# DVE's norm and statistics steps become chunks of their own between the score units, four of them in two halves

## The reference

```python
x = x + tanh(g_xattn[0]) * L0_xattn(layernorm(x), ctx, ctx)   # 16 heads of 8, 512 keys
x = x + tanh(g_ffn[0])   * L0_ffn(layernorm(x))               # 8 experts, top 1, hidden 512
x = x + tanh(g_xattn[1]) * L1_xattn(layernorm(x), ctx)        # self-attention (256 keys), add, norm;
                                                              # cross-attention (512 keys), add, norm;
                                                              # 128 -> 512 -> 128 with relu, add, norm
x = x + tanh(g_ffn[1])   * L1_ffn(layernorm(x))               # rmsnorm, causal self-attention with
                                                              # rotary embedding, rmsnorm, 4 experts, top 2
```

## Time and profile before

| | |
|---|---|
| median of 3 runs | 1208.27 us (1203.97 to 1213.19) |
| the profiled execution's own time | 1199.09 us |
| its span, first to last instruction | 1197.3 us |
| mean granted TensorE clock | 0.941 of full speed |
| PE busy | 1058.3 us (88%) |
| DVE busy | 791.6 us (66%) |
| ACT busy | 620.4 us (52%) |
| POOL busy | 370.3 us (31%) |

### The profile page before, as it was taken

One profiled execution on the slowest core, in us unless ns is written; L12 is line 12 of the kernel. 1 busy time (PEld: TensorE's weight loads), 2 busy tenths in 40 slices (PEclk: granted clock), 3 DMA queues, 4 the chain that ended last, 5 costly groups with the idle time before them and its releaser, 6 DMA issues. The chain is left out here.

```text
span 1197.3 us, 25289 instructions
## 1 busy us (share of the span) xinstructions
PE 1058.3 (88%) x8548; PEld 651.4 (54%) x8548; DVE 791.6 (66%) x1935; ACT 620.4 (52%) x1331; POOL 370.3 (31%) x982
## 2 busy tenths in 40 slices
PE   4999998799998797788899998987988889899998
PEld 1455554477554585444455544444555667656665
DVE  4688887534867424677688869688574776645443
ACT  1477665455664454565477755655544445543221
POOL 4333332221434323434333324322242434200000
PEclk9999998899986898898899998999979899999999
DMA  6655644453434572656655544433334456201000
GB/s 160 192 159 175 176 148 137 153 174 112 130 109 135 161 227 61 192 155 190 193 169 172 158 134 141 136 109 115 106 118 131 125 158 181 75 22 45 10 27 10
DMA packets 173174, 157.98 MB, mean 132 GB/s; under 512 B 13075, under 2 KB 146835, under 8 KB 172691
## 3 DMA queue, kind: packets, MB, share of 16 engines
q1 hardware_dynamic: 168854, 141.24, 39.8%
q0 software_dynamic: 4192, 15.12, 4.0%
HBM read 91.56 MB, written 66.85 MB: 132 GB/s over the span
## 5 line engine op out<-in xcount | busy, mean ns | idle before, releaser
L1102 ACT ACTIVATE prob<-ps 128x512 f32<-128x512 f32 (+1 forms) x768 | 398.9, 578 | 171.5 <-PE ps L1664 128.6
L1296 DVE TENSOR_REDUCE nmax<-ps 128x1 f32<-128x512 f32 x512 | 328.5, 684 | 88.8 <-PE ps L1629 86.8
L1664 PE MATMUL ps<-Qst,Kst 75*128 75x256 bf16 x1408 | 244.4, 285 | 8.6 <-DMA Qst<-mrow 5.8
L1680 PE MATMUL av_ps<-prob,Vx 128*32 128x256 f32 (+1 forms) x3072 | 218.3, 401 | 0.0
L1629 PE MATMUL ps<-Kst,Qst 72*128 72x512 bf16 x512 | 198.2, 403 | 21.7 <-DVE nmax L1296 19.5
L1664 PEld LDWEIGHTS ps<-Qst,Kst 75*128 75x128 bf16 x1408 | 137.0, 102 | 76.4 <-ACT prob L1102 11.8
L1680 PEld LDWEIGHTS av_ps<-prob,Vx 128*32 128x32 f32 x3072 | 92.8, 115 | 67.7 <-issue 38.7
L1026 POOL TENSOR_TENSOR mparts<-nmax,zeros 128x8 bf16<-128x8 f32 x122 | 24.8, 203 | 311.8 <-issue 305.1
L1305 DVE TENSOR_REDUCE nmax<-ps 128x2 f32<-128x512 f32 x128 | 85.9, 687 | 48.5 <-PE ps L1643 47.7
L1106 ACT ACTIVATE OT<-av_ps 128x256 f32<-128x256 f32 x128 | 49.2, 385 | 116.4 <-PE av_ps L1680 116.1
L1629 PEld LDWEIGHTS ps<-Kst,Qst 72*128 72x128 bf16 x512 | 50.5, 99 | 102.2 <-DVE nmax L1296 47.6
(11 more groups left out here) (198 smaller groups left out, 1667.0 us busy)
## 6 DMA issues: line engine op xcount, KB each, us to landing
q_parts<-qp SPq DMA_DIRECT2D x96, 192.0 KB, 2.6
Qst<-q_parts SPq DMA_DIRECT2D x128, 144.0 KB
k_parts<-kp SPq DMA_DIRECT2D x46, 384.0 KB, 3.4
Kst<-k_parts SPq DMA_DIRECT2D x60, 288.0 KB
k_parts<-kp SPq DMA_DIRECT2D x48, 192.0 KB, 2.7
Kst<-k_parts SPq DMA_DIRECT2D x64, 144.0 KB
ctxT<-in_ctxT SPq DMA_DIRECT2D x16, 256.0 KB, 4.8
xs_rows<-in_blank SPq DMA_DIRECT2D x22, 128.0 KB, 4.0
```

What stands on the lines that cost most here:

```text
L1102: act.activation(prob[:, RING_AT[st] % RING, half * 512:half * 512 + w], bank(x)[:, 0:w], ACT.Exp).then_inc(drained(x), 1)
L1296: ve.tensor_reduce(nmax[:, g, u, h % GH:h % GH + 1], bank(st), AX.X, ALU.max, negate=True).then_inc(drained(st), 1)
L1664: last = pe.matmul(o, Ks[0:KROWS, par, h, t * P:t * P + P], Qst[0:KROWS, par, h, :], start=True, stop=not a.rope)
L1680: last = pe.matmul(av_ps[VW * hh:VW * hh + VW, SQ - w:SQ], Vx[:, par, t, h, :], prob[:, place, off * SQ:off * SQ + w], start=(t == 0), sto ...
```

## The change

A second tuple of kinds, `STRINGS`, names the twelve DVE steps above, and `body` opens a chunk at each of them as well. `weave` now has more chunks to place: a string goes to a gap by itself, and the places of the PE steps in the same slot shift too. A step that follows a string and is not of either tuple (a load or a store) goes with the string. Four strings of the feed-forward block become two steps of two tiles each; `f.center` and `f.scale` begin with a `drain`, so each half has one. The arithmetic is the same.

```diff
+STRINGS = ("resid", "stat", "center", "apply", "xstat", "xapply", "f.stat", "f.center", "f.scale", "f.gate", "f.again", "f.rms")
...
         put(n, 14, ("f.stat", i, 0))
-        put(n, 15, ("f.center", i, None))
-        put(n + 1, 0, ("f.scale", i, None))
+        for half in range(2):
+            put(n, 15, ("f.center", i, half))
+        for half in range(2):
+            put(n + 1, 0, ("f.scale", i, half))
...
-        put(n + 1, 5, ("f.again", i, None))
+        for half in range(2):
+            put(n + 1, 5, ("f.again", i, half))
...
-        put(n + 1, 8, ("f.rms", i, None))
+        for half in range(2):
+            put(n + 1, 8, ("f.rms", i, half))
...
             for st in items[p] + [st for st in tiles[0] if st[0] != "m0.h" and per == 1]:
-                if st[0] in MISC_KINDS:
+                if st[0] in MISC_KINDS or st[0] in STRINGS:
                     chunks.append([])
                 chunks[-1].append(st)
...
+            def part_of(t, half):
+                return range(t) if half is None else range(half * t // 2, (half + 1) * t // 2)
...
-            def scale_shift(L, dst, src, shift, t):
-                for i in range(t):
+            def scale_shift(L, dst, src, shift, t, half=None):
+                for i in part_of(t, half):
...
                 elif kind == "f.rms":
                     ve.wait_ge(f_rstd, f_stat(n, 2))
-                    scale_rms(LF, f_out, f_res, "g1", BT).then_inc(f_normed, 1)
+                    last = scale_rms(LF, f_out, f_res, "g1", BT, arg)
+                    if arg == 1:
+                        last.then_inc(f_normed, 1)
```

More of the change, by code:

```diff
@@ L1212, in stats_of, with apply_norm @@
                 return last
-            def apply_norm(L, dst, src, t):
-                for i in range(t):
+            def part_of(t, half):
+                return range(t) if half is None else range(half * t // 2, (half + 1) * t // 2)
+            def apply_norm(L, dst, src, t, half=None):
+                for i in part_of(t, half):
                     last = ve.tensor_scalar(dst[:, i, :], src[:, i, :], L["mv"][:, i, 0:1], L["rstd"][:, i:i + 1],
@@ L1219, in apply_norm, with center_gain @@
                 return last
-            def center_gain(L, dst, src, gain, t):
-                for i in range(t):
+            def center_gain(L, dst, src, gain, t, half=None):
+                for i in part_of(t, half):
                     ve.scalar_tensor_tensor(out=dst[:, i, :], in0=src[:, i, :], scalar=L["mv"][:, i, 0:1],
                                             in1=vecs[:, VI[gain], :], op0=ALU.subtract, op1=ALU.mult)
-            def scale_shift(L, dst, src, shift, t):
-                for i in range(t):
+            def scale_shift(L, dst, src, shift, t, half=None):
+                for i in part_of(t, half):
                     last = ve.scalar_tensor_tensor(out=dst[:, i, :], in0=src[:, i, :], scalar=L["rstd"][:, i:i + 1],
@@ L1232, in scale_shift, with scale_rms @@
                 return last
-            def scale_rms(L, dst, src, gain, t):
-                for i in range(t):
+            def scale_rms(L, dst, src, gain, t, half=None):
+                for i in part_of(t, half):
                     last = ve.scalar_tensor_tensor(out=dst[:, i, :], in0=src[:, i, :], scalar=L["rstd"][:, i:i + 1],
@@ L1508, in ffn_step @@
                     ve.drain()
-                    center_gain(LF, f_res, f_res, "ffn_g", BT)
+                    center_gain(LF, f_res, f_res, "ffn_g", BT, arg)
                 elif kind == "f.scale":
@@ L1512, in ffn_step @@
                     ve.drain()
-                    scale_shift(LF, f_res, f_res, "ffn_b", BT)
+                    scale_shift(LF, f_res, f_res, "ffn_b", BT, arg)
                 elif kind == "f.gate":
@@ L1519, in ffn_step @@
                     ve.wait_ge(f_rstd, f_stat(n, 1))
-                    apply_norm(LF, f_res, f_res2, BT)
+                    apply_norm(LF, f_res, f_res2, BT, arg)
                 elif kind == "f.rms":
                     ve.wait_ge(f_rstd, f_stat(n, 2))
-                    scale_rms(LF, f_out, f_res, "g1", BT).then_inc(f_normed, 1)
+                    last = scale_rms(LF, f_out, f_res, "g1", BT, arg)
+                    if arg == 1:
+                        last.then_inc(f_normed, 1)
             def moe1_step(kind, n, arg):
```

## The result

The changed kernel takes **1230.67 us** (median of five runs, 1220.42 to 1236.06), the kernel before 1208.27 beside it. The ratio is **1.0175, with an interval of 1.0126 to 1.0224**: 1.75% slower, or 21 us. The forecast was a small gain, 1204 us, and the range ended at 1221. The prediction is wrong in its sign.

The account below looks back on a forecast made before the run. PE, busy 88% of the span, was taken as the bound, so only its waits or low-clock time could be won. Gains of 14.3 us less losses of 9.7 made 4.6 us off 1208.27, about 1204 us; own range 1196 to 1210, with rivals 1188 to 1221.

Parts of the forecast that it names:

- The clock: Whole kernel: one stretch at the low clock fewer, as at 197.0, 4 us won; ends 14 us won or lost.
- Gain 1, blocks: Feed-forward blocks: halved strings let reductions come earlier, 4 us; `f.nT` of item 24 behind AV and S, 1.3; together 5.3.
- Gain 2, single strings: Reductions move ahead of single strings, so PE waits less: 3 us in `att1`, 2 in `att0` and `att2`; ends 0 and 15.
- Loss 1, xn: Items 8 to 13: `xapply` waits behind the slot's first reduction, so PE waits longer at `xT`; 4.1 us, ends 0 and 5.
- Loss 2, POOL's queue: Items 10 to 12: later `resid` delays POOL's root, gathers, split and `maxT` by 0.6 us each; 1.8 us lost.
- Loss 3, the copy of V in `att3`: Items 25 to 30, slot 6: `apply` behind a reduction delays V's copy, which `nT` needs; 3.3 us lost, ends 0 and 4.
- Loss 4: Slots 0 and 4 of `att1`: `maxT` moves behind the second S; 0.5 us lost, ends 0 and 2.
- The second, lost cover: Rival: strings lose DVE's idle time under E, with more low-clock stretches in `att1` and `att3`; 19 us slower, 1227 us, chance 0.14.
- The first, waits that only move: Rival: PE waits for DMA landings and POOL in place of banks; gains about 9, losses 9.7; 1209 us, chance 0.22.
- The fourth, all bank waits gone: Rival: all 41.5 us of PE's waits for DVE's score reductions go; 1167 us, chance 0.03.
- The sum: Terms in `att1` without clock: losses 4.1 for xn, 1.8 for POOL's queue, 0.5 for `maxT`, against 3 us gained by single strings.

## Why the prediction was wrong, point by point

- **The clock** is the step that failed. It was taken as 4 us won, one low stretch fewer, because the longest waits become shorter. Measured in the two traces, the time at the low level rose from 141 us to 0.068 / 0.5 x 1218.6 = 166, which costs up to 12 us, and PE's busy time rose by 10.9; over all timed executions the cost is up to 14 to 18 us. The sign of the term was wrong, and with it 16 us or more of the 26 between forecast and result: the term was worked out at one place (197.0, in `att0`), while `att1`, at 0.85 already, has several waits of 0.5 to 1.2 us in each item, and the change made more of them longer than shorter. The upper end, four stretches more or 14 us, holds the traces' 12 but hardly what all executions show.
- **Gain 1, blocks, 5.3 us.** Blocks alone gave 0.9987 (0.9948 to 1.0027), 1.6 us less, and between 6.3 less and 3.3 more: not seen, though an effect of that size isn't quite excluded. Item 22 is not shorter but 1.9 us longer, with DVE busy 35.77 us against 34.89 and the clock at 0.87 against 1.00. Where DVE is nearly saturated, order gave nothing that can be seen. The Trainium skill advises the opposite there (Perfetto Trace Analysis, Optimizing Scalar/DVE Operations: group the work where the engine is saturated). The trace agrees as far as it goes: in halves the item needs 0.9 us more of DVE.
- **Gain 2, single strings, 5 us.** Not found. With `att1` left out, blocks, `att0`, `att2` and `att3` together gave 1.0004 (0.9973 to 1.0035), where the terms without `att1` (gains 7.3, loss 3.3) made 4 us less. In `att1` the bank waits fell by 2.5 us, near the 3 that were taken, but no further than they differ between executions of one order. At the place in item 12 the gain was waited for again at the next landing, as the prediction said of that item and then did not carry through. Whether the other stages gained something that the clock took back (13 us more at the low level, up to 6.5 us) is not clear of the noise.
- **Loss 1, xn, 4.1 us.** The mechanism is as forecast, DVE idle ahead of a reduction with `xapply` behind it, and xn's wait rose by 6.7 us, above the upper end of 5. Its price is another matter: `xapply` alone raised the wait by 4.0 us and cost 0.07% (-0.29 to 0.43).
- **Loss 2, POOL's queue, 1.8 us.** Probably too small: `resid` alone costs 0.64%, some 8 us, and in its trace the parts and landings take 19.7 us of PE's time in `att1`. In the trace of the whole change they rose from 10.1 to 13.6, which is hardly clear of the 13.0 of an unchanged `att1`.
- **Loss 3, the copy of V in `att3`, 3.3 us.** Didn't show: items 24 to 30 went from 172.40 to 168.10. In its place stands what the prediction missed, `apply` at the end of `att1`, behind not one reduction but several (2.48 us): 3.2 us of waits in the whole change and 5 us on item 15; by itself 0.48%, with 3 us on that item.
- **Loss 4** is too small for these traces; all shifts of PE's steps together cost 0.45% (0.16 to 0.74) by themselves.
- **The rivals.** The second, lost cover, at 1227 us with a chance of 0.14, is what happened, with its mechanism and its clock term, in `att1` but not in `att3`. Its test was there to be read, and the earlier trace rows show only one place of it: whether DVE stood idle ahead of most of these strings was not counted. The first, waits that only move, describes the bank waits well and takes in no clock. The fourth, all bank waits gone, would have given 1167 us. The Trainium skill's other rule in the same section, to break up Vector's work where it isn't saturated and makes others idle, met both its conditions here; the measurement, 1.75% slower, speaks against it and decides.
- **The sum** for `att1` as the prediction had it (losses 6.4, gain 3) was 3.4 us; `att1` alone measures 17 us (13 to 21). About two thirds of it is the clock by the traces, and up to 16 us by the granted clock of all its executions.

What stays open: how exactly the loss splits between clock and waits, since low-level time in which PE waits costs less than half of itself; by what pattern of waits the new order of strings lowers the clock; and whether `xapply` really costs more in company than alone.

## What to carry to other kernels

An engine that isn't the bound has useful idle time, and work that stands ahead of a reduction may be in it: before a string is moved behind one, look whether the engine was idle at the string's start, and how many reductions stand there, not one. Trade waits at banks for waits at results only after asking what each is followed by; in item 12 a bank wait won ahead of a landing that was late anyway was worth nothing. And where the bound is TensorE, set the busy time of the same matmuls beside each other first: here half of the loss or more was matmuls that ran at the lower clock, and no table of waits shows that. Do it with more than one execution: the trace with the change everywhere but in `att1`, a kernel as fast as the one before, has PE busy 1082.2 us and 189 us at the low level, both more than the changed kernel's 1069.2 and 166.

## What the hardware showed that I had not expected

Matmuls of the same shape without any idle ahead of them, 256 AV matmuls, took 457, 510 and 385 ns in the same items of three kernels, at granted clocks of 0.85, 0.77 and 0.98, while PE's idle time there was 14.2, 17.7 and 11.3 us. With PE's order kept, idle time did not rise at all (13.9 us), and yet the clock fell to 0.71. The longest wait of PE is no guide either: 1.7 us there, and 3.1 in the same items of the kernel before at 0.85. So neither the sum of PE's waits nor the longest decides; how they lie may, and no run here tests that. The Trainium skill (TensorE: Matmul & The Clock Gate, A second HAM failure mode: psum-queue depth-cycling) tells of a kernel that keeps swinging between the two levels because of frequent small gaps between groups of matmuls, and the trace of the changed kernel agrees: in items 8 to 15 the clock falls 13 times, while PE's longest wait for a reduction is 2.5 us and their mean near 1.

Useless matmuls were cheap where the clock was low. 384 of them for `att1`'s items, at 16.4 / 120 = 0.137 us of busy time each, are some 52 us of PE's time; the kernel before got 0.72% slower by them, 9 us, and items 12 to 15 of the changed kernel 8 us shorter. With 108 in fewer items the kernel before was not slower (0.9976, 0.9938 to 1.0014).
